# Two LayerNorms that only centre, on ScalarE, with the reciprocal deviations applied later

## The reference, cut to what matters

```python
def _layernorm(x, eps=1e-05):
    return (x - mean(x)) / sqrt(var(x) + eps)

# attention: 32 heads of 16
q = layernorm(x) @ Wq ; k, v = split(ctx @ Wkv)
q, k = rope(q, pos), rope(k, pos)
w = softmax(q @ k.T / 4) ; x1 = x + (w @ v) @ Wout + bout
# feed-forward
y = layernorm(x1) ; xn = y * rsqrt(mean(y * y) + eps2) * norm_w
logits = xn @ Wc.T / max(temperature, 0.1)
top 32 of 1024 logits -> softmax -> expressed = weights @ genes
out = x1 + tanh(expressed @ Wd.T) * xn * (expressed @ Wu.T) * scale
```

## Time and profile before

| | |
|---|---|
| median of 3 runs | 527.66 us (527.11 to 529.24) |
| the profiled execution, its own time | 528.95 us |
| its span, first to last instruction | 527.0 us |
| TensorE busy | 457.6 us (87%) |
| VectorE busy | 416.1 us (79%) |
| ScalarE, POOL busy | 258.1, 262.2 us (49%, 50%) |
| mean granted TensorE clock | 0.946 of full |

### The profile page before, as it was taken

How to read it: one execution, slowest core, us unless ns; L and a number is a source line. 1 busy time by engine, 2 the same in 40 slices (tenths; PEclk the granted TensorE clock), 3 DMA queues, 4 the chain that set the end, 5 groups by cost and what they waited for, 6 DMA issues and landing times. The chain is left out here.

```text
span 527.0 us, 10932 instructions
## 1 busy us (share of the span) xinstructions
PE 457.6 (87%) x3866; PEld 336.8 (64%) x3866; DVE 416.1 (79%) x644; ACT 258.1 (49%) x386; POOL 262.2 (50%) x263
## 2 busy tenths in 40 slices
PE   1727698999999999999999999999999999796734
PEld 0525465677776767676777777777677776565523
DVE  3574274989898989899998989898989897866680
ACT  2641626374737374645555463647464737243111
POOL 0453527282919292928374655647382919110111
PEclk9967699999999999999999999999999999979776
DMA  7940504141322314050505050505041321200000
GB/s 266 283 90 18 95 1 89 25 87 26 69 64 51 84 30 103 21 109 21 109 21 109 21 109 21 109 9 113 9 92 38 73 59 37 65 23 1 21 20 21
DMA packets 81754, 34.45 MB, mean 65 GB/s; under 512 B 73136, under 2 KB 75200, under 8 KB 81728
## 3 DMA queue, kind: packets, MB, share of 16 engines
q1 hardware_dynamic: 80768, 33.05, 27.1%
q10 hardware_dynamic: 960, 1.05, 0.6%
HBM read 12.86 MB, written 4.19 MB: 32 GB/s over the span
## 5 line engine op out<-in xcount | busy, mean ns | idle before, releaser
L830 DVE MAX8 top<-stage_b 128x8 f32<-128x1024 f32 x64 | 78.0, 1218 | 32.3 <-ACT stage_b L579 32.1
L396 POOL TENSOR_TENSOR rstd<-var,minus_half 128x1 f32<-128x1 f32 x16 | 8.8, 550 | 178.1 <-DVE var L804 178.1
L838 DVE MATCH_REPLACE8 stage_b<-top,stage_b 128x1024 f32<-128x1024 f32 x64 | 77.3, 1208 | 0.0
L367 POOL TENSOR_TENSOR stage_b<-stage_b,cos_t 128x512 f32<-128x512 f32 x32 | 41.2, 1288 | 37.0 <-issue 25.5
L994 PE MATMUL gene<-wcT_h,yT_h 128*128 128x512 f32 x128 | 53.9, 421 | 1.1 <-DVE yT_l L817 1.1
L994 PE MATMUL gene<-wcT_l,yT_h 128*128 128x512 f32 x128 | 51.8, 405 | 0.0
L994 PE MATMUL gene<-wcT_h,yT_l 128*128 128x512 f32 x128 | 51.6, 403 | 0.0
L1101 PE MATMUL dense<-stage_a,v_ext 128*32 128x128 f32 x1024 | 42.6, 287 | 2.8 <-ACT stage_a L552 2.1
L536 ACT ACTIVATE parts<-turned 128x1024 f16<-128x1024 f32 x32 | 33.8, 1057 | 19.1 <-POOL turned L380 19.1
L765 DVE TENSOR_REDUCE row_max<-score_a 128x8 f32<-128x1024 f32 x32 | 38.9, 1217 | 4.8 <-PE score_a L1060 4.8
L765 DVE TENSOR_REDUCE row_max<-score_b 128x8 f32<-128x1024 f32 x32 | 38.9, 1215 | 3.7 <-PE score_b L1060 3.5
(11 more groups left out here) (149 smaller groups left out, 1129.2 us busy)
## 6 DMA issues: line engine op xcount, KB each, us to landing
x_ring<-x_dram SPq DMA_DIRECT2D x16, 256.0 KB, 2.6
out_dram<-x_ring SPq DMA_DIRECT2D x16, 256.0 KB, 2.5
ctx_sb<-ctx_dram SPq DMA_DIRECT2D x16, 128.0 KB, 2.5
stage_a<-L_ffn_Wc_dram SPq DMA_DIRECT2D x1, 2048.0 KB, 10.1
stage_b<-L_xattn_Wq_dram ACTq DMA_DIRECT2D x1, 1024.0 KB, 5.9
stage_b<-L_xattn_Wkv_dram SPq DMA_DIRECT2D x1, 1024.0 KB, 9.3
stage_b<-L_xattn_Wout_dram SPq DMA_DIRECT2D x1, 1024.0 KB, 12.5
genes_sb<-L_ffn_genes_dram SPq DMA_DIRECT2D x2, 256.0 KB, 5.2
```

The costliest lines, as they stand in the source:

```text
L367: pool.tensor_tensor(halves(qk_cos), halves(qk_sb), trig(cos_t, t), ALU.mult).then_inc(s_cosm[n], 1)
L830: nc.vector.max(top[:, 8 * n:8 * n + 8], logit if n == 0 else rest).then_inc(s_top[n], 1)
L838: nc.vector.match_replace(rest, top[:, 8 * n:8 * n + 8], logit if n == 0 else rest, REMOVED).then_inc(s_rem[n], 1)
```

## The change

Both LayerNorms only subtract the mean, and ScalarE does it: `center_x` and `center_y` write mean - x (scale -1, bias mean), so the sign is turned, and Wq, wc_scale and up_scale are negated to turn it back. The reciprocal deviations are applied where the results are read: rstd1 scales `read_q`, rstd2 scales `read_logits` and the kept copy. `center_x` stands in ScalarE's order behind `e_hi`, `center_y` between `ctx_hi` and `y_hi`; VectorE loses `norm1_apply` and `norm2_apply`.

```diff
-            def norm1_apply(t):
-                dve.wait_ge(s_rstd1, t + 1)
...
-                nc.vector.tensor_scalar(xn[:], slot(t), mv1[:, 0:1], rstd1[:], ALU.subtract,
-                                        ALU.mult).then_inc(s_xn, 1)
...
-            def norm2_apply(t):
-                dve.wait_ge(s_norm2, t + 1)
...
-                nc.vector.tensor_scalar(yn[:], slot(t), mv2[:, 0:1], rstd2[:], ALU.subtract,
-                                        ALU.mult).then_inc(s_yn, 1)
...
+            def center_x(t):
+                hold(act)
+                act.wait_ge(s_mv1, t + 1)
+                if not first(t):
+                    act.wait_ge(s_xT, t)
+                nc.scalar.activation(xn[:], slot(t), ACT.Identity, bias=mv1[:, 0:1], scale=-1.0).then_inc(s_xn, 1)
...
+            def center_y(t):
+                hold(act)
+                act.wait_ge(s_mv2, t + 1)
+                if not first(t):
+                    act.wait_ge(s_yT, t)
+                    act.wait_ge(s_kept, t)
+                nc.scalar.activation(yn[:], slot(t), ACT.Identity, bias=mv2[:, 0:1], scale=-1.0).then_inc(s_yn, 1)
...
+                act.wait_ge(s_rstd1, t + 1)
+                nc.scalar.activation(qk_sb[:, 0:DIM], bank("q"), ACT.Copy, scale=rstd1[:]).then_inc(s_q_sb, 1)
...
+                act.wait_ge(s_norm2, t + 1)
+                nc.scalar.activation(logit[:, n * 512:(n + 1) * 512], logit_bank[n], ACT.Copy,
+                                     scale=rstd2[:]).then_inc(s_lgr[n], 1)
...
-                pool.tensor_copy(kept_of(t), yn[:]).then_inc(s_kept, 1)
+                pool.tensor_tensor(kept_of(t), yn[:], rstd2[:].broadcast_to([P, DIM]), ALU.mult).then_inc(s_kept, 1)
```

ScalarE's iteration:

```diff
                     read_wT(t4, 0)
                     e_hi(t4)
+                if later(t0, 1):
+                    center_x(t0)
                 if t2 is not None:
                     attn_hi(t2)
...
                     read_q(t0)
                     ctx_hi(t0)
                 if t2 is not None:
+                    center_y(t2)
                     y_hi(t2)
```

Further parts of the same change. The load of Wkv is cut in two, and the splits of the weights before the first tile go piece by piece, keys first:

```diff
-            sp.dma_start(wkv_raw, wkv.rearrange("(k p) n -> p k n", p=P)).then_inc(s_wkv, 16)
+            for n, (to, landed) in enumerate(((wk_raw, s_wk), (wv_raw, s_wv))):
+                sp.dma_start(to, wkv[:, n * DIM:(n + 1) * DIM].rearrange("(k p) n -> p k n", p=P)).then_inc(landed, 16)
...
+            trig_tables()
+            center_x(0)
+            for k in range(CK):
+                wk_hi(k)
+            for k in range(CK):
+                wv_hi(k)
+            for k in range(XK):
+                wq_hi(k)
             ctx_hi(0)
             x_hi(0)
             read_k(0)
             wout_hi()
             read_q(0)
+            center_x(1)
             read_v(0)
```

TensorE drops waits that others imply, and `transpose_o` waits for each half of oT on its own:

```diff
             def transpose_o(t):
-                pe.wait_ge(s_oT[0], t + 1)
-                pe.wait_ge(s_oT[1], t + 1)
-                pe.wait_ge(s_ex[2], t + 1)
                 for n in range(8):
-                    last = nc.tensor.transpose(score_b[:, n * P:(n + 1) * P], oT_sb[:, n * P:(n + 1) * P], ident[:])
+                    if n % 4 == 0:
+                        pe.wait_ge(s_oT[n // 4], t + 1)
+                    last = nc.tensor.transpose(pair("o")[:, n * P:(n + 1) * P], oT_sb[:, n * P:(n + 1) * P], ident[:])
```

`express` takes the second half of the gene weights first; its first wait is still for the half that is read last. POOL waits in `ln1` and `ln2` until the deviation of the tile before has been used. The PSUM tensors are now named by use; in the loop every use keeps its banks. SP and VectorE compute the loop's tile numbers into registers at the start of an iteration:

```diff
             with eng.Fori(lags + 1, TILES) as i:
+                for n in counts:
+                    eng.to_reg(i - n)
...
-            run(sp, 6, iteration)
+            run(sp, 6, iteration, range(0, 6))
...
-            run(dve, 6, iteration)
+            run(dve, 6, iteration, range(1, 6))
```

More of the change, by code:

```diff
@@ L229, in first, with only, upto, run @@
             return isinstance(t, int) and t == 0
+        def only(t, *tiles):
+            return isinstance(t, int) and t in tiles
+        def upto(t, tile):
+            return not (isinstance(t, int) and t > tile)
         def hold(eng):
             eng.wait_ge(s_trig, 1)
-        def run(eng, lags, iteration):
+        def run(eng, lags, iteration, counts=()):
             def tiles(i):
@@ L943, in iteration @@
                     find_top(t3, 2)
+            angles()
+            constants()
+            norm1_stats(0)
+            for k in range(CK):
+                wk_lo(k)
+            for k in range(CK):
+                wv_lo(k)
+            ctx_lo(0)
+            for k in range(XK):
+                wq_lo(k)
             x_lo(0)
@@ L949, in _ @@
             scale_up()
-            norm1_apply(1)
-            wcT_lo(1)
-            for k in range(2, 4):
+            for k in range(1, 4):
                 wcT_lo(k)
@@ L1003, in transpose_x @@
                 pe.wait_ge(s_xn, t + 1)
-                if isinstance(t, int) and t == 1:
-                    pe.wait_ge(s_q_sb, 1)
-                elif not first(t):
+                if later(t, 1):
                     pe.wait_ge(s_aT_l, t - 1)
+                if only(t, 1):
+                    pe.wait_ge(s_split_wcT, 3)
                 for k in range(XK):
-                    last = nc.tensor.transpose(dense[:, k * P:(k + 1) * P], xn[:, k * P:(k + 1) * P], ident[:])
+                    last = nc.tensor.transpose(bank("xT")[:, k * P:(k + 1) * P], xn[:, k * P:(k + 1) * P], ident[:])
                 last.then_inc(s_xT, 1)
@@ L1013, in transpose_ctx @@
                 pe.wait_ge(s_ctx, (t + 1) * 16)
-                if isinstance(t, int) and t == 1:
-                    pe.wait_ge(s_k_sb, 1)
-                elif not first(t):
+                if later(t, 1):
                     pe.wait_ge(s_x1, t - 1)
                 for k in range(CK):
-                    last = nc.tensor.transpose(dense[:, 512 + k * P:512 + (k + 1) * P],
-                                               ctx_sb[:, k * P:(k + 1) * P], ident[:])
+                    last = nc.tensor.transpose(bank("ctxT")[:, k * P:(k + 1) * P], ctx_sb[:, k * P:(k + 1) * P], ident[:])
@@ L1064, in transpose_max @@
             def transpose_max(t):
-                for g in range(GROUPS):
-                    pe.wait_ge(s_mx[g], t + 1)
-                nc.tensor.transpose(score_a[:, 0:P], row_max[:], ident[:]).then_inc(s_rmT, 1)
+                pe.wait_ge(s_mx[2], t + 1)
+                pe.wait_ge(s_mx[3], t + 1)
+                nc.tensor.transpose(bank("row_maxT")[:, 0:P], row_max[:], ident[:]).then_inc(s_rmT, 1)
             def scoresT(t, g):
@@ L1130, in transpose_y @@
+                if later(t, 1):
                     pe.wait_ge(s_tanh, t - 1)
+                if only(t, 1):
+                    pe.wait_ge(s_lgr[0], t)
                 for k in range(XK):
-                    last = nc.tensor.transpose(gene[:, k * P:(k + 1) * P], yn[:, k * P:(k + 1) * P], ident[:])
+                    last = nc.tensor.transpose(bank("yT")[:, k * P:(k + 1) * P], yn[:, k * P:(k + 1) * P], ident[:])
                 last.then_inc(s_yT, 1)
             def logits(t, n):
-                pe.wait_ge(s_yT_h, t + 1)
@@ L1137, in logits @@
-                pe.wait_ge(s_yT_l, t + 1)
-                if first(t):
-                    pe.wait_ge(s_split_wcT, 4)
-                if n == 1 and (not isinstance(t, int) or t >= 2):
-                    pe.wait_ge(s_t2, t - 1)
-                three_pass(gene[:, n * 512:(n + 1) * 512], (yT_h, yT_l),
+                if n == 0:
+                    pe.wait_ge(s_yT_l, t + 1)
+                elif n == 1:
+                    if later(t, 1):
+                        pe.wait_ge(s_t2, t - 1)
+                    if only(t, 1):
+                        pe.wait_ge(s_lgr[1], t)
@@ L1153, in transpose_w @@
+                for g in range(4):
+                    last = nc.tensor.transpose(wT_bank[n][:, g * P:(g + 1) * P],
+                                               gene_w[:, n * 512 + g * P:n * 512 + (g + 1) * P], ident[:])
                 last.then_inc(s_wT[n], 1)
@@ L1240, in _ @@
             wcT(0)
-            pe.wait_ge(s_v_sb, 1)
             wcT(1)
```

394 lines of the change are left out of this document (206 added, 188 removed).

## The result

| | before | after |
|---|---|---|
| median | 528.18 us (527.11 to 529.24, 4 runs) | 535.23 us (533.56 to 535.68, 4 runs) |
| the profiled execution | 528.95 us | 535.42 us |
| TensorE, VectorE, ScalarE busy | 87, 79, 49% | 84, 73, 53% |

The two were measured side by side: the ratio is 1.0128, with a 95% interval of 1.0096 to 1.0159. The change makes the kernel 7.05 us slower; +6.05 was predicted.

The account below looks back on a forecast made before the run. TensorE was taken to set the period (busy 27.20 of 27.65 us). Twelve full tiles at 0.82 (+9.8), early tiles +0.4 and -0.5, start -1.0, last tiles -2.65 sum to +6.05: 533.7 us, range 529.8 to 539.7.

Parts of the forecast that it names:

- 1.19 late: Full tile: transpose_y waits for center_y and starts at about 324.42 instead of 323.23, up to 1.3 late.
- 0.46 is waiting for VectorE's row maximum and the context's low part: Full tile, 323.23 to 324.78: 0.46 of TensorE's 1.55 us is waiting for things that will be ready first.
- I take +1.05, bounds 0.9 and 1.4: Full tile: the next scores group, waiting for the negated maximum's small DMA, comes 1.05 us later.
- I take 0.23 back: Full tile, split transpose_o and express: earlier transposes and an earlier gene read give back 0.23 us, bounds 0 and 0.4.
- ...that slack covers it: First centring: attn_hi some 0.35 late, covered because the output projection asks for aT_l about 1 us after it is ready.
- the fourth rival: Both centrings: Identity needs another activation table, loads cost 36 us more, about 570; chance 0.02.
- -1.0: The start: key weights ahead of value weights bring the first scores earlier by 1.0 us, bounds 0 and -1.5.
- If the key halves are done before 11.4: The start: on this condition value halves and queries end by 14.8 instead of 15.9; key projection starts at 15.7.
- -2.65: Last two tiles, without query projection: yn comes sooner as variance, POOL's power and VectorE's pass leave the path; 2.65 us less.
- the third rival: TensorE's clock: each new stall lowers it, some 3 us more per tile, about 575; chance 0.03. Reverse: 1.9 back.
- Recovery: Full tiles: small holes downstream absorb the late yn, a tile pays about 0.1, total 525.1; chance 0.10.
- A costlier stall: Full tiles: SP's register steps and a later DMA restart add 0.5 per tile, total 539.7; chance 0.10.

Follow-up runs that it names:

- y_early: The changed kernel with center_y moved ahead of the query read and context read in ScalarE's queue; 527.90 us, ratio 0.9979 to the kernel before.
- twice_early: `both_early` with the second centring issued twice, first into a spare tile that nobody reads; 527.36 us, ratio 0.997 to the kernel before.
- wT_between: `both_early` with ScalarE's read of the second half of the transposed gene weights put between the two reads of oT; 520.47 us, ratio 0.9856.
- x_early: The changed kernel with center_x moved ahead of e_hi in ScalarE's queue; 532.19 us, ratio 1.0063 to the kernel before.
- before_center: The kernel before with the centring alone, scaled reads and copy included; loads, start splits, TensorE's waits and transpose_o as before; 537.72 us, ratio 1.0193.
- both_early: The changed kernel with center_y ahead of the query read and center_x ahead of e_hi; 523.06 us, ratio 0.9891 to the kernel before.

## Why the prediction was right

**The stall, its size and place.** "1.19 late": 1.18. "center_y starts at 323.36 + 0.38 - 0.10", "0.71": in the rows above 357.07 is 0.28 behind 356.79, and it takes 0.71. The length of an instruction form that no row showed (Identity with a bias pointer) came out of a neighbour of the same engine and a difference of widths; the scaled read (0.69), taken from the tanh, likewise. The kernels `y_early` and `twice_early` show that it is the place.

**"0.46 is waiting for VectorE's row maximum and the context's low part".** It was 0.57. From the start of down_up's last matmul to the key projection are 0.26 when nothing is waited for, and I had taken 0.36 (0.23 and 0.13 for the row maximum's transpose).

**"I take +1.05, bounds 0.9 and 1.4" for the DMA chain.** 1.18 - 0.57 + 0.26 = 0.87, just under the lower bound. In the rows above the DMA is issued at 361.25, 3.42 behind the transposes' start (before 3.71, rows 2 and 4), so 0.29 of the 1.18 are made good and it is 0.89 late, and the scores follow 2.20 behind it. The chain's 0.94 was good; what I had put on top for the 0.25 and for SP's register steps was not there.

**"I take 0.23 back".** This step failed, within its bounds (0 and 0.4). transpose_o did start 0.34 sooner, and at express it was all lost again. What failed is "would end about 0.2 sooner":

```profile
371.15 1.04 PE L1175 MATMUL psum<-ident,stage_b 128*128 128x128 f32 x8
371.29 1.08 ACT L652 ACTIVATE stage_a<-psum 128x512 f32<-128x512 f32 x2
372.43 2.05 PE L1237 MATMUL psum<-stage_a,genes_sb 128*128 128x128 f32 x16 [0.23 <-ACT stage_a L652]
```

The two gene reads end at 372.37 and express starts 0.06 later, as before (310.60 and 310.65, rows 5): ScalarE still does them behind both reads of oT, and transposes that start sooner don't move them. `wT_between` shows it from the other side: with one of the two reads put ahead, 0.38 of the 1.27 go.

**"...that slack covers it", of the first centring.** This step failed too, and it is the largest error in a full tile: +0.28. I looked for who reads aT_l (the output projection) and not for who waits for its bank (the transposes of x, 0.57 + 0.33 us earlier in TensorE's order). `x_early` shows that it is this wait: there it is gone, and the one for yn (1.08) is not.

**VectorE's slack, the scaled copy and the table.** VectorE's 28 us less bought nothing, as said. The scaled copy takes 1.04 (the plain one 0.75), and nothing in the full tiles waits for it. There are two table loads in the profile after, as in the one before, so the fourth rival is out. The Trainium skill, "ScalarE: Activation LUTs", "Table sets: the hidden batching unit", says that identity is in every set; this trace agrees.

**Per full tile** that makes, with the table's -0.09 and the -0.04 at the transposes of attn, 0.87 + 0 + 0.28 - 0.09 - 0.04 = +1.02, and +1.00 by the period, for 0.82 predicted: two misses of the same sign as each other (0.23 and 0.28) and two of the other (0.18 and 0.13). Over twelve tiles the error is 1.6 us.

**The start.** "-1.0" is near the -1.48 found, but by another way, so the step is wrong. The key projection starts at 16.43, not 15.7, and the first scores at 39.14, not 38.3:

```profile
2.14 1.41 SPq L307 DMA_DIRECT2D stage_b<-L_xattn_Wkv_dram  x2
10.97 1.22 ACT L506 ACTIVATE wkv_h<-stage_b 128x512 fp32r<-128x512 f32 x2 [2.14 <-DMA stage_b<-L_xattn_Wkv_dram]
21.89 1.92 ACT L524 ACTIVATE wout_h<-stage_b 128x2048 fp32r<-128x2048 f32 x1 [1.90 <-DMA stage_b<-L_xattn_Wout_dram]
39.14 0.61 PE L1123 MATMUL psum<-kT,qT 64*128 64x128 f16 x8 [8.18 <-DMA kT<-parts]
```

"If the key halves are done before 11.4" assumed that half a load lands in about half the time. The keys' half was there at 10.97, 0.46 ahead of the whole load before (11.43, rows 7). The output weights' split, taken as unchanged, started at 21.89 instead of 21.01. What came to the first scores was 0.15. The other 1.3 came behind them, with the clock: with the scores at the same time, the half-clock stretch lasted from 34.1 to 44.3 where before had 30.2 to 47.3. That was not foreseen, and that the two numbers are near each other is luck. Ten kernels here have the halved load and the new order of the splits; in their profiles the half-clock stretch lasts from 10.2 to 17.1 us, and the first row maximum comes between 47.80 and 49.10, that is 0.35 to 1.65 earlier than before. Their keys' splits begin at 10.69 to 11.14; in the two kernels with the whole load they begin at 11.43 (before) and 12.14 (`before_center`). So the load seems to give something, but no run took it alone.

**The last two tiles.** "-2.65" against -3.24 measured (1.93 + 1.31). TensorE's idle ahead of the two transposes fell from 3.17 and 3.73 to

```profile
469.06 0.66 PE L1199 MATMUL psum<-ident,yn 128*128 128x128 f32 x4 [1.87 <-ACT yn L622]
494.45 0.72 PE L1199 MATMUL psum<-ident,yn 128*128 128x128 f32 x4 [2.42 <-ACT yn L622]
```

which is 1.30 and 1.31 less, as the step had it. (Its own differences, 460.94 - 459.65 and 488.37 - 487.1, make 2.56 and not 2.65.) The other 0.63 isn't parted. What the third rival called its reverse fits: the half-clock stretch at the first of them lasted 3.4 us (471.0 to 474.4) instead of 6.8 (460.3 to 467.1). But from the last transposes of y to the end after takes 0.49 more (39.14, before 38.65), with 27.1 us at half clock instead of 24.4.

**The sum was nearer than its terms.** Against the profiled execution's +6.6, the sum of +6.05 was 1.6 too low in the full tiles and 1.1 too high in the rest: at the start by 0.5, in the next two intervals by 0.1, at the end by 0.6. That these nearly cancel is luck; the mechanism that carries the forecast, the wait for yn, is not.

**The rivals.** Recovery fell: the wait for yn is on the path in every tile. A costlier stall (0.5 more per tile) fell: it was 0.2 more. The clock stayed at 1.00 through the new stalls of 1.08.

**The rule of the skill.** The Trainium skill, "ScalarE: Activation LUTs", section "Rules for kernel authors", puts adds and products on VectorE and gives its advantage per element, up to about three times, for bf16; this kernel is fp32. The prediction left that condition out, and it took VectorE's 1.10 for the length of its pass. With no instruction of POOL beside it the pass took 0.48, ScalarE's 0.71, so in this the trace agrees with the rule; beside POOL's `gate` it took 1.10, and then ScalarE is the quicker one. Neither decided this case: centring cost the same per tile on either engine (28.01 and 28.03) wherever it was done before TensorE asked.

## What to carry to other kernels

A step moved to a less busy engine is paid by what stands ahead of it in that engine's queue: look for the idle stretch there, and put it ahead of the instruction that waits for the bound engine, not behind. When a result comes later, ask who waits for its buffer as well as who reads it. The first and last tiles lack the work that hides things in the middle, and are to be summed apart; there a wait that is 0.6 us longer came with a loss of four, most of it with the clock, and the clock's part could not be forecast. And the length that one row shows for an instruction can hold a wait for another engine: look at the same instruction where that engine is idle.

## Of the hardware

- Near-equal kernels differ by several microseconds in how long TensorE's half-clock stretches last at both ends of the run. Behind the same wait of 2.42 us ahead of the last transposes of y, the half clock lasted 6.8 us in five traces, 3.4 in `wT_between`, and did not come in `both_early` and `before_center`. Of `both_early`'s 5.4 us on before, 5.3 lie in the last interval and behind it, in these stretches and in shorter waits; the runs don't part the two.
- Two half loads took SP's queue 1.41 us to issue in after, one whole load 0.89 in before.
- A pass of VectorE over 128x512 (fp32, SBUF to SBUF) took 0.48 us alone with the mean as its only operand per row and 0.54 with mean and deviation; either took 1.10 where an instruction of POOL ran beside its first 0.82.
